# One pool of seven PSUM banks for score and maxima tiles of attention, with K loads moved ahead and spare matmuls

## Time and profile before

| | |
|---|---|
| median of three runs | 3381.76 us (3369.64, 3383.88, 3381.76) |
| the profiled execution | 3366.61 us, span 3364.9 us |
| TensorE busy, mean granted clock | 87% of the span, 0.733 |
| VectorE, ScalarE, GpSimd busy | 59%, 43%, 11% |
| first attention, stage from / first exponential / last | 75 / 154.7 / 883 us |
| second attention (causal) | 1007 / 1056.9 / 1674 us |
| third attention (causal) | 1960 / 2009.9 / 2629 us |
| the rest: norms, projections, experts, local attention, feed-forward | between and after these |

### The profile page before, as it was taken

One profiled execution on the slowest core, in us unless ns is written; L12 is line 12 of the kernel. 1 busy time (PEld: TensorE's weight loads), 2 busy tenths in 40 slices (PEclk: granted clock), 3 DMA queues, 4 the chain that ended last, 5 costly groups with the idle time before them and its releaser, 6 DMA issues. The chain is left out here.

```text
span 3364.9 us, 40017 instructions
## 1 busy us (share of the span) xinstructions
PE 2913.9 (87%) x14544; PEld 1293.3 (38%) x14544; DVE 1972.5 (59%) x3987; ACT 1435.5 (43%) x2105; POOL 360.0 (11%) x544
## 2 busy tenths in 40 slices
PE   4799999999645999999859849999999598979897
PEld 2333334333213433443334324333433245634563
DVE  3698898986155654665245447645654265535554
ACT  1177676765411345344512203454345324632463
POOL 1000001000010000100100010001000133303330
PEclk8599999997765555555569965555555698988898
DMA  5000000000020000000000020000000012301230
GB/s 197 23 22 8 20 9 22 10 7 2 18 75 39 14 18 11 26 9 5 6 14 0 0 77 22 7 20 31 6 8 3 30 38 91 104 18 38 86 109 18
DMA packets 73403, 106.03 MB, mean 32 GB/s; under 512 B 23704, under 2 KB 46232, under 8 KB 71576
## 3 DMA queue, kind: packets, MB, share of 16 engines
q1 hardware_dynamic: 69856, 92.15, 8.1%
q10 hardware_dynamic: 3384, 11.74, 0.9%
HBM read 51.17 MB, written 17.17 MB: 20 GB/s over the span
## 5 line engine op out<-in xcount | busy, mean ns | idle before, releaser
L684 ACT ACTIVATE att_probs<-psum 128x1024 f32<-128x1024 f32 (+3 forms) x1152 | 1039.2, 951 | 1029.0 <-PE psum L728 1028.5
L637 DVE TENSOR_REDUCE att_part_max<-psum 128x1 f32<-128x512 f32 x1792 | 1133.2, 683 | 397.9 <-PE psum L710 396.8
L710 PE MATMUL psum<-att_k_rows,att_q_rows 34*128 34x512 f32 (+3 forms) x2304 | 982.3, 602 | 132.0 <-DMA att_k_rows<-att_ones 63.1
L710 PEld LDWEIGHTS psum<-att_k_rows,att_q_rows 34*128 34x128 f32 x2304 | 464.8, 252 | 971.0 <-DVE att_part_max L637 575.7
L753 PE MATMUL psum<-att_probs,v_aug 128*9 128x512 f32 (+3 forms) x3712 | 648.7, 786 | 15.6 <-ACT att_z_sb L676 15.6
L728 PE MATMUL psum<-att_q_rows,att_k_rows 34*128 34x512 f32 (+3 forms) x2304 | 564.6, 511 | 12.2 <-DMA att_q_rows<-att_max_rows 8.8
L634 DVE CUSTOM_DVE_ANT_0 att_masked<-psum,mask_max_sb 128x384 bf16<-128x384 f32 (+3 forms) x512 | 235.4, 486 | 261.6 <-PE psum L710 260.3
L728 PEld LDWEIGHTS psum<-att_q_rows,att_k_rows 34*128 34x128 f32 x2304 | 341.9, 264 | 93.7 <-ACT att_probs L684 47.4
L590 POOL TENSOR_SCALAR_AFFINE_SELECT att_probs<-att_probs 128x256 f32<-128x256 f32 x256 | 102.9, 408 | 1242.7 <-ACT att_probs L684 1240.5
L1334 ACT ACTIVATE latt_probs<-psum,latt_bias,latt_scale 128x192 f32<-128x192 f32 x256 | 127.5, 507 | 122.2 <-DVE latt_bias L1373 122.2
L749 PE MATMUL psum<-att_probs,att_one_only 128*9 128x512 f32 (+3 forms) x1280 | 158.5, 569 | 10.6 <-ACT att_z_sb L676 10.5
(11 more groups left out here) (254 smaller groups left out, 2549.9 us busy)
## 6 DMA issues: line engine op xcount, KB each, us to landing
att_k_rows<-k_pieces SPq DMA_DIRECT2D x48, 256.0 KB
latt_k<-local_k_T SPq DMA_DIRECT2D x32, 384.0 KB, 3.0
att_q_rows<-q_pieces SPq DMA_DIRECT2D x168, 64.0 KB
lproj_table<-in_tables SPq DMA_DIRECT2D x16, 512.0 KB, 3.6
latt_q<-local_q_T SPq DMA_DIRECT2D x32, 256.0 KB, 2.4
latt_v_own<-local_v_tok SPq DMA_DIRECT2D x32, 256.0 KB, 2.3
k_pieces<-proj_piece SPq DMA_DIRECT2D x12, 512.0 KB, 2.8
q_pieces<-proj_piece SPq DMA_DIRECT2D x12, 512.0 KB, 2.7
```

What stands on the lines that cost most here:

```text
L637: nc.vector.tensor_reduce(column, ring[e % NRING][:, 0:w], AX.X, ALU.max).then_inc(ring_free, 1)
L684: nc.scalar.activation(probs[s % NPROBS][:, pr, :, at:BANK], st[pr][:, :, at:BANK], ACT.Exp, scale=scale).then_inc(st_free, 1)
L710: nc.tensor.matmul(ring[e % NRING][:, 0:w], q_rows[u % NQ][rows, pr, qt * P:(qt + 1) * P].bitcast(F32R), k_rows[g % 2][rows, pr, kc * BANK ...
```

## The change

- **One pool.** Banks 0 to 6 are given out in the order of issue, round and round, to score tiles (one bank each) and maxima tiles alike. `Plan.owners` lists who takes which slot, and a matmul waits until the owner seven places back has been read: by VectorE (`ring_free`) if that was a maxima tile, by ScalarE (`st_free`) if it was a score tile. Where the two banks of a pair are not neighbours (the pool wraps) the exponential is split in two instructions.
- **Order.** Half of a step's maxima tiles now stand between its two score pairs and half behind the second pair; the products come last in the step.
- **Spare matmuls.** `keep_busy` multiplies the identity with 256 columns of `x_T` into `z_ps`, whose contents are overwritten later: once after each of the last five pairs of opening tiles, three times before the first step, three times in each of the first two steps (which have no products). The memset of `z_ps` and its semaphore go.
- **K loads.** Three K buffers. K of the second group is loaded ahead of `put_max(0)`, K of the third ahead of `put_max(1)`, K of the fourth at the end of group 0. The masked scratch tile has four buffers and a wait of its own.
- **Weights.** The experts' `w13`, `w2` and the local attention's `w_in`, `w_v`, `w_out` share one buffer of 3 MB. The latter three are loaded on ScalarE's queue in a block after the experts, and waited for in a block after the third attention.

The order of the units is the same before and after.

```diff
-NRING = 3
+NSLOT = 7
+NK = 3
+WARM = 256
...
 class Plan:
+        self.k_loads = []
+        self.k_load_of = []
+        for g, c in self.units:
+            if not self.k_loads or self.k_loads[-1] != g:
+                self.k_loads.append(g)
+            self.k_load_of.append(len(self.k_loads) - 1)
...
+        self.owners = []
+        self.slot_of = {}
+        done = self.take_maxima(0, self.issued_by(0, 0))
+        for n, (u, kb) in enumerate(self.steps):
+            for pr in range(2):
+                for i in range(2):
+                    self.take(("scores", n, pr, i))
+                done = self.take_maxima(done, self.issued_by(u, (kb + (pr + 1) / 2) / self.blocks[u]))
...
 attention(), SyncE
             load_q(2)
             zero_max(2)
+            load_k(1)
+            set_ones(1)
             put_max(0)
             load_q(3)
             zero_max(3)
             for u, (g, c) in enumerate(units):
+                if u == 0:
+                    load_k(2)
+                    set_ones(2)
                 if u + 1 < NU:
                     put_max(u + 1)
-                if u == 0:
-                    load_k(1)
-                    set_ones(1)
...
-                if last_of_group and g + 2 < NG:
-                    load_k(g + 2)
+                if more_k:
+                    load_k(n + NK)
...
 attention(), ScalarE
-                    nc.scalar.activation(probs[s % NPROBS][:, pr, :, at:BANK], st[pr][:, :, at:BANK], ACT.Exp, scale=scale).then_inc(st_free, 1)
+                    mine, a, b = probs[s % NPROBS], slot(("scores", s, pr, 0)), slot(("scores", s, pr, 1))
+                    if b == a + 1:
+                        both = bank(psum, a, 2).rearrange("p (i q) -> p i q", i=2)
+                        nc.scalar.activation(mine[:, pr, :, at:BANK], both[:, :, at:BANK], ACT.Exp, scale=scale).then_inc(st_free, 1)
+                    else:
+                        nc.scalar.activation(mine[:, pr, 0, at:BANK], bank(psum, a)[:, at:BANK], ACT.Exp, scale=scale)
+                        nc.scalar.activation(mine[:, pr, 1, at:BANK], bank(psum, b)[:, at:BANK], ACT.Exp, scale=scale).then_inc(st_free, 1)
...
 attention(), TensorE
+            def slot_is_free(n):
+                if n >= 0:
+                    kind, *which = plan.owners[n]
+                    if kind == "maxima":
+                        pe.wait_ge(ring_free, which[0] + 1)
+                    else:
+                        pe.wait_ge(st_free, 2 * which[0] + which[1] + 1)
...
-                        if e >= NRING:
-                            pe.wait_ge(ring_free, e - NRING + 1)
+                        slot_is_free(n - NSLOT)
...
-                if s > 0:
-                    pe.wait_ge(st_free, 2 * (s - 1) + pr + 1)
                 for i in range(2):
+                    n = plan.slot_of[("scores", s, pr, i)]
+                    slot_is_free(n - NSLOT)
...
+            def keep_busy(n):
+                at = n % 2 * WARM
+                nc.tensor.matmul(z_ps[:, at:at + WARM], ident, x_T[:, 0:WARM], start=True, stop=True, skip_group_check=True)
+
+            opening = plan.issued_by(0, 0)
+            for count in range(2, opening + 1, 2):
+                maxima(count)
+                if count > opening - 10:
+                    keep_busy(count // 2)
+            maxima(opening)
+            for n in range(3):
+                keep_busy(n)
             for s, (u, kb) in enumerate(steps):
                 if kb == 0:
                     pe.wait_ge(m_in[u % NQ], MIN_ * (u // NQ + 1))
                 scores(s, 0)
+                maxima(plan.issued_by(u, (kb + 0.5) / plan.blocks[u]))
                 scores(s, 1)
-                maxima(plan.issued_by(u, (kb + 0.5) / plan.blocks[u]))
+                maxima(plan.issued_by(u, (kb + 1) / plan.blocks[u]))
                 if s >= 2:
                     products(s - 2)
-                maxima(plan.issued_by(u, (kb + 1) / plan.blocks[u]))
+                else:
+                    for n in range(3):
+                        keep_busy(n)
...
 forward()
-        late = held(ctx, "w_in", "w_v", "w_out", "pair_rows", "pair_spread", "bands", "w_up", "b_up", "w_down")
+        weights = sb("weights", [P, 6 * 1024])
+        late = held(ctx, "pair_rows", "pair_spread", "bands", "w_up", "b_up", "w_down")
...
+        late["w13"] = weights[:, 0:4096].rearrange("p (e f) -> p e f", e=NE)
+        late["w2"] = weights[:, 4096:6144].rearrange("p (e n h) -> p e n h", e=NE, n=2)
...
+        with nc.Block() as block:
+            @block.scalar
+            def _(act):
+                for n, b in local.items():
+                    act.dma_start(full(b), a[n]).then_inc(local_in, 16)
...
+        with nc.Block() as block:
+            @block.sync
+            def _(sp):
+                sp.wait_ge(local_in, 16 * len(local))
```

87 lines of the change are left out of this document (50 added, 37 removed).

## The result

The changed kernel takes **3445.97 us** (median of 4 runs, 3443.72 to 3446.91) against 3375.70 us for the kernel before (4 runs, 3350.79 to 3383.88). The ratio is 1.022 with a 95% interval of 1.016 to 1.028: slower by about 70 us; the interval is clear of 1, and leaves open whether the change is above 2%. Forecast were 3510 us, slower with a chance of 0.77, and a range of 3330 to 3660. So the side is right, the time lies in the range, and the size was about twice too large (143 us for 77 between the profiled executions).

The account below looks back on a forecast made before the run. VectorE's reductions with three maxima banks held the first attention, TensorE at half clock the causal ones. Terms: +77 first attention, +62 both causal, +4 weights; +143 on 3366.6 gave 3510 us, range 3330 to 3660.

Parts of the forecast that it names:

- The step of the first attention: First attention, units 0 to 13: each of 224 steps goes from 2.69 to 3.09 us, +90 us in all.
- The chain: Within one step: scores, exponential, last maxima matmul waiting for it, products, next scores; 3.09 us at full clock, 4.46 at half.
- Unit 14: First attention's unit 14: no new wait; between -21 us if it keeps its clock and 0, taken as -15.
- Causal units 3 and 11: Causal attentions: steps lengthen from 3.89 to 4.46 us at half clock, less on the diagonal; +8 us in each unit.
- Causal units 1, 2, 9 and 10: Causal attentions: steps already as long as the new chain, so 0; ends -5 and +5 for units 0-2 and 8-10 together.
- The K loads: Causal attentions: K loads ahead of max rows delay first scores +13 us and unit 1 +5; wait ahead of unit 9 goes, -3.
- The spares: Spare matmuls in the attentions' openings and first steps: +2 us in the first attention, 0 in the causal ones.
- Shared weights: Ahead of the third attention: 3 MB loaded after the experts and two more blocks that drain all engines, +4 us.
- (1): The pool frees TensorE in the first attention, so units run at VectorE's pace; 3335 us, faster, chance 0.10.
- (2): The clock stays up in the causal attentions, -152 us each; 3174 us, chance 0.08.
- (3): The first attention loses its clock too, for half of 224 steps, +153 us; 3663 us, chance 0.17.
- (4): All small: chain costs half (+44), unit 14 gains 21, causal +62 met by units at full clock; 3390 us, chance 0.05.

Follow-up runs that it names:

- e9: Changed kernel with its pool kept but the old order within a step (both score pairs, maxima, products, maxima); 3380.6 us.
- e2: Changed kernel with the products moved between the two pairs of maxima tiles in each step, pool kept; 3374.4 us.
- e1: Changed kernel with fixed banks again instead of the pool, its new order, spare matmuls and K loads kept; 3490.3 us.
- e5: Changed kernel with fixed banks and the products ahead of the second pair of maxima tiles; 3496.9 us.
- e4: Changed kernel without its spare matmuls, z's bank set to zero by VectorE again; 3446.3 us.
- e3: Changed kernel with the second and third groups' K loads both behind unit 1's max rows on SyncE's queue; 3444.9 us.
- e6: Changed kernel with products between maxima pairs except in causal units 0-2 and 8-10, K loads behind unit 1's and unit 2's max rows, no spares; 3287.6 us.
- e10: As e6, with ScalarE's copy of z one exponential earlier; 3268.7 us.
- e11: As e10, with spare matmuls placed in causal steps: one or two a step in units of 8 or more blocks, five more in six units' second step; 3081.3 us.
- e12: As e11, with ScalarE's copy of z back in its old, later place; 3314.1 us.
- e7: As e6, with one spare matmul in each causal step, ahead of its first scores; 3450.2 us.
- e8: As e7, with two spare matmuls in each causal step, one ahead of each pair of scores; 3416.0 us.

## Why the prediction was right and where it was wrong

**The step of the first attention: right.** The chain came out at 3.08 us for 3.09, with the wait at the matmul that was named, clock 1.00. VectorE's share fell from 89% to just under 80% (564.56 of 708.20). The term of +90 measured +78.5, 0.35 for 0.40 a step on average, since about one step in ten has no wait. The wait itself is 0.50 us for the 0.8 named. But the reason was given under the pool, and the pool is only half of it. e9 has the same pool, the old order and no cost; e2 has the pool, the split scores and no cost; e1 has the order and no pool and costs 3.4 us a unit for the 5.4. With the pool the cost belongs to the products standing behind both maxima pairs, and the wait is for ScalarE; with three fixed banks it comes with the split of the score pairs, wherever the products stand (e1, e5), and the wait is for VectorE. (The fixed banks in the old order are the kernel before, without the other parts of the change; e9 has these parts and takes 44.9 us, so they cost nothing in these units.) The prediction wrote the order down (s s M M s s M M) and did not price it by itself.

**Unit 14: right, by luck**, -19.6 for -15. The term was a bet between two outcomes and named no cause. e4 shows that the spares have no part in it (41.0 us without them), e1 and e9 that neither the pool nor the new order by itself is what does it (40.7 with fixed banks and the new order, 43.6 with the pool and the old one). In the kernel before the clock fell 1.0 us after a wait of 0.93 us for the copy of z; the changed kernel waits 0.97 us at the same place and keeps it. Why is open.

**Causal units 3 and 11: mis-sized**, +4.4 each for +8. The chain itself is right. In unit 3 the products follow each other at 4.41 us for the forecast 4.46:

```profile
1259.77 1.89 PE L796 MATMUL psum<-att_probs,v_aug 128*9 128x512 f32 x8
...
1264.18 1.89 PE L796 MATMUL psum<-att_probs,v_aug 128*9 128x512 f32 x8
```

The mean of the unit's 16 steps is 4.17 (66.70 / 16), so not all of them pay it.

**Causal units 1, 2, 9 and 10: the step that failed.** They were put at 0 with ends of -5 and +5 for all six. They gained 3.6, 3.1, 3.3 and 2.9 us, 13 per attention. Here a step has more than four tiles, and the deeper maxima buffer pays: under the same order unit 1 takes 40.4 us with three banks and 35.4 with the pool. The prediction had compared two chains and not the depth of the buffer. The pool needs the new order for it: with the old one unit 1 takes 38.1 us (e9). Together with units 3 and 11 (-7) and unit 8 (-6 for -3), this makes 23 us, and the other units take 1 to 2 back; between the forecast +31 and the measured +9.4 of the second attention lie 21.6. The third had +3.1, as its units 6 and 7 got some microseconds of full clock (21.5 and 11.8 us for 24.5 and 12.6).

**The K loads: right by the sum.** +13 forecast and +13.5 measured at the first exponential; +5 forecast at unit 1's max rows and +5.3 measured in unit 0 (27.0 us for 21.7, and 27.1 in e4, so it is not the spares). What the prediction did not see is that the cure would be as dear as the illness (e3): a K load costs wherever it stands ahead of a due transfer of max rows, and two in a row cost 11 us at unit 2.

**The spares: mis-sized in the first attention**, where they cost 10 us (e4) for the forecast 2, since the opening is on the path there. 0 in the causal ones is right.

**Shared weights: 0 for +4.** Between the second and the third attention, where three of them are now loaded, the stretch is 1.4 us longer (267.9 for 266.5), and the first attention begins 4.3 us earlier (70.9 us for 75.2), perhaps since less is loaded at the start; no run tests this part alone. The stretch behind the third attention was 5.1 us longer in this profile, but 716.4 and 716.0 us in e4 and e2, which have the shared weights too, and 716.7 before.

**The rivals.** (1) falls: the exponential holds the bank as long as the rows said. In e2, where other work stands ahead of the waiting matmul and the wait is gone, a unit takes 45.1 us and not the rival's 41.5, so a freed TensorE would not have brought VectorE's bound either. The faster kernels with this pool (e6, e10, e11) have their gain elsewhere. (2) did not occur: the causal clock stayed at 0.51. The reason given for this, an idle TensorE at the first scores, is not borne out: in e10 the K load is out of the way and TensorE is busy 99% of the attention, and the clock is 0.51 all the same. The price fits: in e11, where the clock holds in most units (0.88 and 0.86), the causal attentions take 105 and 98 us less than in e10, for the 152 of the rival at full clock throughout. (3) did not occur; the longer step kept full clock through 14 units. The Trainium skill, TensorE: Matmul & The Clock Gate (section "A second HAM failure mode: psum-queue depth-cycling"), says that short idle times between groups of matmuls, as a kernel cycles through PSUM banks, make the clock swing. In the first attention the trace does not bear that out: 199 waits of 0.5 us and a clock of 1.00. In e12 the clock does swing, but by waits for the copy of z, one in a unit, and not by the cycling of banks. (4) is closest of the rivals in size (3390, 56 us off, where the forecast is 64 off), for other reasons: the chain's cost was near its full price. The forecast of +143 is 66 us over the profiled +77.1: 11.5 from the steps of the first attention, 4.6 from unit 14, 21.6 and 27.9 from the two causal attentions, 4 from the weights, less 3.7 for the rest of the first attention (+2 forecast, +64.6 - 78.5 + 19.6 = +5.7 measured).

## What to carry to other kernels

Count what an in-order engine does between two hand-overs to each consumer. If one block of it is longer than the tiles that are outstanding keep the consumer busy, the order is slow. Here the changed order was slow with both ways of giving out the banks; moving the products between the maxima pairs was worth 5.3 us a unit with the pool and nothing with three fixed banks. Order and depth of the buffers have to be chosen together. A transfer that isn't due yet costs whatever is due behind it on the same queue, so put it directly behind the urgent one, one at a time. At half the clock, look for the one wait that loses the clock before adding work to hold it: here spares alone brought nothing or cost time (e12, e7 and e8 against e6), the copy moved by one exponential brought 19 us, and both together 6% (e6 to e11).

## What was not expected of the hardware

Removing a wait changed far more than its length. In e12 a wait of 1.13 us at the start of a unit was followed within 2 us by a fall of TensorE's clock from 2.4 to 1.2 GHz, and the unit took 65.1 us for 41.6. It is no rule: after five waits of the same kind out of fifteen the clock stayed. In the first attention of the changed kernel waits of 0.5 us in almost each step left the clock at 1.00. In the causal attentions TensorE was busy 99% of the time at 1.2 GHz (583.38 of 587.60 us in e10) and hardly ever got 2.4 GHz. With 210 matmuls more per attention (2735 for 2525), all of them useless, it was granted 0.88 and the attention took 105 us less.
